# Products that nobody reads in five waits of TensorE, in a two-layer graph attention kernel

## What is computed

```python
h = jnp.maximum(_layernorm(x, axis=-1), 0.0)
x = x + _L0_gnn_ref(h, adj, ...)   # h W, tanh, source and destination scores, leaky, masked softmax,
                                   # values, elu, then gate*feat + (1-gate)*h, gate = sigmoid(h Hw.T + Hb)
h = jnp.maximum(_layernorm(x, axis=-1), 0.0)
x = x + _L1_gnn_ref(h, ..., adj)   # q, k, v, masked softmax(q k.T / 8) v, times Wf, plus bf
```

## Time and profile before

| what | value |
|---|---|
| median of 3 runs | 956.3 us (953.92 to 956.41) |
| profiled execution | 958.36 us, its span 956.6 us |
| PE (TensorE matmul) busy | 915.2 us, 96% |
| DVE (VectorE) busy | 790.9 us, 83% |
| ACT (ScalarE) busy | 607.8 us, 64% |
| POOL (GpSimd) busy | 213.0 us, 22% |
| mean granted clock | 0.986 of full speed |
| PEclk in 40 slices | 9998999999999999999999999999999999999979 |

### The profile page before, as it was taken

The page is one execution under the profiler, slowest core; times in us unless marked ns, Lnnn a source line. Parts: engine busy times, 40 slices in busy tenths (PEclk is TensorE's granted clock), DMA queues, the critical chain, the costliest instruction groups (busy, mean ns, idle before and its releaser), DMA issues.

```text
span 956.6 us, 24708 instructions
## 1 busy us (share of the span) xinstructions
PE 915.2 (96%) x9851; PEld 816.6 (85%) x9851; DVE 790.9 (83%) x1513; ACT 607.8 (64%) x1277; POOL 213.0 (22%) x297
## 2 busy tenths in 40 slices
PE   4888999999999999999999999999999999999788
PEld 4676988979798897989989798998979899897777
DVE  3897979889887988889898888988888898887915
ACT  3746658575775847668485856848486684847532
POOL 4205040140504104050320405022040502204020
PEclk9998999999999999999999999999999999999979
DMA  9303252151525305152340525234052522403203
GB/s 225 77 1 35 35 101 36 39 79 20 101 35 93 43 34 73 31 101 35 79 57 20 83 35 101 36 80 55 12 91 36 101 35 76 54 8 67 35 1 100
DMA packets 185124, 56.40 MB, mean 59 GB/s; under 512 B 166450, under 2 KB 185012, under 8 KB 185012
## 3 DMA queue, kind: packets, MB, share of 16 engines
q1 hardware_dynamic: 185012, 54.83, 32.7%
HBM read 17.07 MB, written 12.58 MB: 31 GB/s over the span
## 4 chain that ended last, share of the span: by engine, by line
issue 48%; PE 27%; POOL 14%; DVE 5%; ACT 4%; DMA 1%; SPq 0%; POOLq 0%; ACTq 0%; DVEq 0%
POOL x_in L501 6%; PE ps L814 4%; PE ps L828 4%; POOL x_in L507 4%; PE ps L830 4%; PE ps L829 4%; ACT p L529 3%; PE ps L906 3%; POOL rstd L469 2%; PE ps L907 2%; PE ps L910 2%; PE ps L1029 1%; PE ps L1046 1%; PE ps L985 1%; POOL shift L472 1%
## 5 line engine op out<-in xcount | busy, mean ns | idle before, releaser
L464 POOL TENSOR_SCALAR ve<-mv 128x4 f32<-128x4 f32 x32 | 7.7, 239 | 639.2 <-DVE mv L1120 638.0
L501 POOL TENSOR_TENSOR x_in<-x_in,bf_row 128x384 f32<-128x384 f32 x64 | 83.9, 1344 | 43.1 <-ACT p L529 43.1
L1264 DVE COPY_PREDICATED_SCALAR z<-not_adj,masked 128x768 f32 x64 | 70.0, 1093 | 25.7 <-ACT z L627 25.7
L1130 DVE TENSOR_TENSOR hT1l<-ps,hT1h 128x384 fp32r<-128x384 f32 x124 | 61.0, 551 | 21.2 <-ACT hT1h L534 20.5
L590 ACT ACTIVATE ps<-hb_all 128x384 f32<-128x384 f32 x56 | 27.8, 496 | 73.0 <-DVE x_in L1276 73.0
L608 ACT ACTIVATE QT<-ps,bq_col 128x512 f32<-128x512 f32 x48 | 33.0, 688 | 63.0 <-PE ps L910 63.0
L1115 DVE BATCH_NORM_STATS2 stats<-x_in 128x6 f32<-128x384 f32 x128 | 64.6, 547 | 7.3 <-DMA x_in<-in_x_dram 7.3
L507 POOL TENSOR_TENSOR x_in<-x_in,h 128x384 f32<-128x384 f32 x64 | 65.1, 1048 | 9.8 <-DVE Wf_lo L1160 9.8
L828 PE MATMUL ps<-Wv_hi,hT1h 128*128 128x384 f32 x192 | 66.5, 346 | 0.0
L828 PE MATMUL ps<-W_hi,hT0h 128*128 128x384 f32 x192 | 65.7, 342 | 0.0
L829 PE MATMUL ps<-W_lo,hT0h 128*128 128x384 f32 x192 | 65.3, 340 | 0.0
(11 more groups left out here) (139 smaller groups left out, 2696.1 us busy)
## 6 DMA issues: line engine op xcount, KB each, us to landing
x_in<-in_x_dram SPq DMA_DIRECT2D x16, 768.0 KB, 5.1
V<-v_tok SPq DMA_DIRECT2D x64, 192.0 KB, 5.7
V<-v_tok SPq DMA_DIRECT2D x128, 96.0 KB, 2.4
out_dram<-x_in SPq DMA_DIRECT2D x15, 768.0 KB, 3.6
out_dram<-x_in SPq DMA_DIRECT2D x4, 192.0 KB, 1.9
QT<-in_L_gnn_W_dram SPq DMA_DIRECT2D x3, 192.0 KB, 5.8
x<-in_L_gnn_H_w_dram SPq DMA_DIRECT2D x1, 576.0 KB, 5.5
thT<-in_L_gnn_Wq_dram SPq DMA_DIRECT2D x1, 576.0 KB, 5.1
```

The source lines that it names most:

```text
L501: pool.tensor_tensor(x_in[:, j % 3, t], x_in[:, j % 3, t], bf_row[:], ALU.add).then_inc(x2_biased, 1)
L1130: return dve.tensor_tensor(to[:, :, toks], ps[:, job(name, g, t) % BANKS, 0:D].rearrange("p (c m) -> p c m", m=P), high[:, :, toks].bitcas ...
L1264: dve.copy_predicated(zu, not_adj[:, tiles].unsqueeze(2).broadcast_to((P, 2, PAIRS0, N)), masked0[:].unsqueeze(2).unsqueeze(3).broadcast_t ...
```

## The change

Five groups of matmuls are added to TensorE's program, and nothing else is changed. Their results are not read: each goes into a bank whose next job starts it afresh. Ahead of the turns of group 0's h stand 30 float32 products of the identity with itself (128 columns). The other groups take the bank of the job that follows (the same wait as that job's) and make products of a high half of W0 with another (384 columns): 10 before the turns of group 1's h in pass 0, 12 before the first turns of layer 1 in pass 1, 14 between `attend1(1)` and the output product in pass 15, 16 before the first turns of layer 1 in pass 16.

```diff
             pe.wait_ge(consts_made, 8)
 
+            def unused_products(n, name, g, k):
+                dst = take(name, g, k)[:, 0:D]
+                for _ in range(n):
+                    pe.matmul(dst, wh["W0"][:, 0, 0:P], wh["W0"][:, 1], start=True, stop=True)
+
+            for _ in range(30):
+                pe.matmul(ps[:, hw_bank(0), 0:P], ident[:], ident[:], start=True, stop=True)
+
             def turn_hw():
...
                 if i == 0:
+                    unused_products(10, "h0_low", 1, 0)
                     turn_h0(1, 1, range(TILES))
+                if j == 0:
+                    unused_products(12, "h1_low", 0, 0)
+                if j == last:
+                    unused_products(16, "h1_low", last, 0)
                 if real(j):
                     turn_tokens("h1_low", h1_made, xn1_turned, lambda t, c: p1_tile(t)[:, c * P:(c + 1) * P], j)
...
                     turn_probs1()
                     attend1(0)
                     attend1(1)
+                    unused_products(14, "out_made", j, 0)
                     output(j, (hT0h, hT0l), (0, 1))
```

## The result

The changed kernel takes 950.3 us (median of 9 runs, 948.31 to 952.45) beside 957.4 us for the kernel before (9 runs): a ratio of 0.993, 95% interval 0.9918 to 0.9942. So 6.7 us are gone, 5.5 to 7.9. The forecast was 952.5 us from 956.3, 3.8 us less. The profiled execution of the changed kernel took 948.31 us, its span 946.5; the mean granted clock is 1.000, before it was 0.986.

A forecast was written before the change was run, and what follows sets the result against it. TensorE was taken as the bound from 140 to 860 us. The terms 2.0 + 1.1 + 1.4 + 0.0 + 0.5 = 5.0 us gave 951.3 us from the 956.3 median; 952.5 was taken, range 949.2 to 956.4.

The forecast's parts named there:

- Launch: 30 identity products before the first turns of h: faster turns and products behind them, a gain of 2.0 us.
- The gaps of the fast turns: At launch, the clock may fall in gaps between fast turns, leaving a gain of 0.9 us.
- The slower rival: The 30 launch products do not raise the clock and end at 16.1 us: 957 to 960 us in all; chance 6%.
- First pass: 10 products before the turns of pass 1's h: faster turns and records, VectorE starts sooner, a gain of 1.1 us.
- Second pass: 12 products before layer 1's first turns: first Wq product sooner and six of them faster, a gain of 1.4 us.
- this risk for the sum: Unprofiled runs may have shorter slow stretches, so less to give back: 952.5 us taken, not 951.3 at full carry.
- Pass 15: 14 products before pass 14's output: it ends 1.7 us sooner, but VectorE reads it later anyway; value nought, bounds 0 and 0.2.
- Last pass: 16 products before the last first turns: Wq products start later but run faster, a gain of 0.5 us.
- I expect 1.2 GHz: In the last pass, the 16 products start slow because TensorE has been idle since 906.2 us.
- The time passes to 897 us unchanged: After the second pass's group TensorE is the bound, so the time gained carries to 897 us unchanged.
- Turns that do not hold the clock: Rival: groups ahead of turns warm nothing that comes after; 1.7 us gained in all, 954.6 us; chance 8%.
- A cover partly lost: Rival: clock falls in gaps of the first turns and the last group runs slow; 2.2 us, 954.5 us; chance 20%.

The follow-up runs named there:

- The two runs of the tail: The kernel before with only the 14 and 16 products added before pass 14's output and the last first turns, or the 16 alone: ratios 0.9983 and 0.9988.
- the one filled otherwise: Changed kernel with 15 products into bank 2 in pass 1, 18 more behind pass 14's output and 6, not 16, behind the output sum: 948.54 us.

## Why the prediction came out as it did

The direction and the mechanism were right, and the measured 950.3 us lies in the range given. The measured difference, 6.7 us, is larger than the 3.8 us between forecast and median and the 5.0 us of the sum. The part of it that the forecast's mechanism gives is 4.3 us, as worked out below; the rest came from a place that the forecast had left out, and it is luck that the range held it too. By its steps:

- *Launch, 2.0 us.* Measured 2.2 us over the profiles. The end of the group was put at 11.7 us; it came at 11.2 to 12.0. The gaps of the fast turns did not lose the clock in any of four profiles. The slower rival, products that do not raise the clock, is out: the 60 records took 8.9 to 9.7 us, of the 13.8 that all slow would take.
- *First pass, 1.1 us.* Measured 1.0 us.
- *Second pass, 1.4 us.* Mis-sized. The working of the stage was right to 0.1 us against the one profile, but in that profile the slow stretch behind this wait lasted into the products with Wq, as in three of the nine without the group; in two more the clock fell for the turns alone, and in four not at all. Averaged over executions the term is some 0.3 us. The step that failed is the choice of the one execution as the base; I had named this risk for the sum and priced it at 1.2 us in total, which is about what this term lost.
- *Pass 15, nought.* The two runs of the tail agree with it within their intervals.
- *Last pass, 0.5 us between a loss of 0.9 and a gain of 2.7.* From the first block product of pass 15 to the first product with Wk, the five profiles with the group need 49.8 to 52.6 us, mean 51.0, the eight without and without the refilled wait 51.8 on average: 0.8 us, from a gain of 2.0 to a loss of 0.8. "I expect 1.2 GHz" was right for one profile of the changed kernel and wrong for the other.
- *"The time passes to 897 us unchanged."* This step failed. The four terms as measured give 2.2 + 1.0 + 0.3 + 0.8 = 4.3 us, an estimate from few profiles, and 6.7 (5.5 to 7.9) were measured. In the profiles, the stretch from the 24 records of pass 2 to those of pass 15 takes 729.1 to 733.7 us in the six with standstills (mean 731.5) and 727.3 to 729.5 in the eight without (mean 728.5). That division is made by the outcome: the two profiles of the kernel before alone need 731.3 and 729.1 us, the two of the changed kernel 729.1 and 728.8, 1.2 us less on average. Between 1.2 and 3 us of that kind are of the size of the 2.4 that are missing.
- *Rivals.* Turns that do not hold the clock: 12 turns ran at 2.4 GHz with gaps between them at launch and again in pass 0 and 1, and the gain behind them arrived. The page cited for it, "TensorE: Matmul & The Clock Gate", Part 4, of the Trainium skill, says that full speed does not engage in transposes; the trace disagrees for turns that come behind products (1.95 us of work in 3.00 at launch, clock 1.00). Whether turns alone could raise the clock, no run here shows. A cover partly lost: it is what happens in the tail in some executions, beside a sum that came out higher for another reason.
- *Sums in the forecast that do not come out.* The rival with the cover partly lost gives 956.3 - 2.2 = 954.1 us, not 954.5. The low end of the range by its own words (2.0 to 2.6 us at launch, 0.5 to 2.7 in the tail) is 951.3 - 2.8 = 948.5 us, not 949.2. In the slower rival 18 slow products from 19.5 us would end at 25.4 us, not 24.1. None of the three decides anything here: the measured time lies in the range either way, and the slower rival is out.

**What stays open.** What makes TensorE stand still in the second attention, and why in some executions and not in others (3.5 and 1.0 us in the two profiles of the kernel before). Where it stands still, the traces show. Count what TensorE's trace records, weight loads, matmuls and semaphore waits alike: from pass 2 to pass 14 each pass has 1278, which is 5 x 256 - 2. All 27 standstills of over 0.15 us between the small products, in six profiles, stand at the same place in this count of 256: the remainder is 193, and 194 in the run with 64 small products at launch. So they come one product (two records) later in each pass: in front of product 78 in pass 4, shown above, and of product 88 in pass 14. The kernel before, the run with 64 small products at launch and the one with 5 in pass 0, all three in pass 14:

```profile
839.75 1.64 PE L1046 MATMUL ps<-KT,V 64*64 64x64 f32 x87
841.93 0.46 PE L1046 MATMUL ps<-KT,V 64*64 64x64 f32 x9 [0.53 <-issue]
```

```profile
839.83 1.70 PE L1054 MATMUL ps<-KT,V 64*64 64x64 f32 x88
842.28 0.46 PE L1054 MATMUL ps<-KT,V 64*64 64x64 f32 x8 [0.75 <-issue]
```

```profile
837.21 1.51 PE L1055 MATMUL ps<-KT,V 64*64 64x64 f32 x77
839.31 0.56 PE L1055 MATMUL ps<-KT,V 64*64 64x64 f32 x19 [0.60 <-issue]
```

5 small products are 20 records, and the standstills stand 10 products earlier. In the changed kernel and the one filled otherwise, with 163 and 169 records more ahead of pass 2, the place has moved into the turns behind the small products, and the short standstills there (7 in three profiles) have the remainder 193 to 195. The Trainium skill, Runtime: NRT & Kernel Launch, Instruction fetch mechanics, says that the program is fetched in blocks of 256 instructions and that this is hidden by the pace of issue. The trace agrees with the length of the block, and shows up to 1.2 us that were not hidden. So the place is shown, and the run with 5 small products does not speak against it, though its expectation failed: any instructions ahead of pass 2 do not do away with the standstills, they move them. That it is the fetch which falls behind is argued from the place and the length alone. And the place does not decide whether TensorE stands still: with the same 20 records, one profile has three standstills and one has none, and with the place 22 or 60 products earlier three profiles have none.

The times say about as much. Take from each measured gain the terms of the groups in it, as worked out above: 0.9 to 3.1 us are left in the seven kernels whose profiles have at most 0.3 us of standstills (launch group, 10 products, 12 products, 30 small ones, no launch group, changed kernel, and the one filled otherwise, whose tail is 2.3 us shorter by the same stretch), and 0.8, 0.4 and -0.5 us in the two of the tail and the one with 64 small products. The interval of each is 1.1 to 1.5 us either way. The run with 5 small products is the exception: 4.9 us are left, with 2.6 us of standstills in its profile, and nothing on record explains it. So some 2 us of the 6.7 have a place and a likely cause, which is not shown.

## What to carry to other kernels

A short wait of TensorE can cost more behind it than in it: look at the granted clock behind each wait (here those of 2.7 to 3.4 us mattered), and in more than one profile, since the same wait loses the clock in one execution and keeps it in the next. Filling such waits with products into a bank that the next job starts afresh is cheap where the products can begin at once and end before the work is ready; a filler that itself waits for the bank's reader begins late, can run slow and then stands in front of ready work. So choose a bank that is free when the wait begins, not the one that the next job happens to use. And when instructions are added ahead of a long row of small products, look whether a standstill in that row has moved: it changes the time by as much as a stage's clock does, and would be credited to the wrong step.

## What was not expected of the hardware

- Waits of 3.03 and 3.33 us kept 2.4 GHz, waits of 2.93 and 3.17 us lost it, in like places of the same kernels. The length of the wait did not decide between 2.9 and 3.4 us.
- 60 records of float32 products of 128 columns took 8.86 us at launch, where the clock rose on the way, and 60 of 32 columns 3.41 us, 57 ns each.
- 96 small products in a row, 1.73 us, stood still for up to 1.2 us with nothing awaited, in some passes and some executions and not in others, and each time at the same place in a count of 256 of TensorE's recorded instructions (remainder 193 or 194).
